# A graph-attention kernel whose walk over destination rows takes edge tiles column by column, one transfer for each step

## The reference

```
h_proj = einsum('nd,rde->rne', h, relation_weight)
t_r, h_r = h_proj[etype, src], h_proj[etype, dst]
att = sum(t_r * tanh(h_r + efeat), axis=-1)
a = segment_softmax(att, dst)
h_nb = segment_sum(h[src] * a[:, None], dst)
out = leaky_relu((h + h_nb) @ res_w1.T) + leaky_relu(h * h_nb @ res_w2.T)
x = layernorm(x + out)
```

## Time and profile before

| | |
|---|---|
| median of 3 runs | 8692.76 us (8691.06 to 8694.27) |
| the profiled execution's time | 8697.39 us |
| its span, first to last instruction | 8695.6 us |
| prologue, up to the first gather | 0 to 452 us |
| far chunks (gathers of sources and destinations) | 452 to 4009 us |
| near chunks (gathers of sources) | 4009 to 6211 us |
| node stages and second layer | 6211 to 8696 us |
| busy: PE, PEld, DVE, ACT, POOL | 59%, 54%, 73%, 38%, 59% |

### The profile page before, as it was taken

One profiled execution on the slowest core, in us unless ns is written; L12 is line 12 of the kernel. 1 busy time (PEld: TensorE's weight loads), 2 busy tenths in 40 slices (PEclk: granted clock), 3 DMA queues, 4 the chain that ended last, 5 costly groups with the idle time before them and its releaser, 6 DMA issues. The chain is left out here.

```text
span 8695.6 us, 134675 instructions
## 1 busy us (share of the span) xinstructions
PE 5099.5 (59%) x44411; PEld 4652.1 (54%) x44577; DVE 6318.7 (73%) x6282; ACT 3267.4 (38%) x4027; POOL 5097.0 (59%) x5165
## 2 busy tenths in 40 slices
PE   6657777777777777775000000000159999999995
PEld 2247676766766766774000000000158888888884
DVE  4546556556565565566777787777789999999997
ACT  3312122122122222222222222222257777777772
POOL 3777777777777777777777777777631121111114
PEclk8855555555555555555555555555559999999996
DMA  9978877878788777887444444444310000000001
GB/s 390 383 170 184 183 179 179 179 180 182 178 180 183 176 180 184 176 181 170 132 132 133 132 132 133 130 134 130 94 35 10 10 9 10 9 10 10 9 10 31
DMA packets 1216488, 1142.57 MB, mean 131 GB/s; under 512 B 993596, under 2 KB 1047422, under 8 KB 1203200
## 3 DMA queue, kind: packets, MB, share of 16 engines
q1 hardware_dynamic: 1036607, 754.44, 34.3%
q0 software_dynamic: 160592, 281.30, 14.7%
q10 hardware_dynamic: 19200, 105.87, 3.1%
HBM read 697.83 MB, written 444.96 MB: 131 GB/s over the span
## 5 line engine op out<-in xcount | busy, mean ns | idle before, releaser
L1543 POOL DMA_INDIRECT gs<-table,idx_s x3125 | 3011.1, 964 | 981.3 <-issue 964.5
L1851 PEld LDWEIGHTS banks<-win,pick 128*125 128x125 f32 x9900 | 2151.1, 332 | 341.5 <-issue 316.1
L1851 PE MATMUL banks<-win,pick 128*125 (+1 forms) x9900 | 2120.9, 413 | 190.9 <-DVE pick L1599 189.0
L765 ACT CAST columns<-ps_u 128x784 bf16<-128x784 f32 x1968 | 1577.8, 813 | 461.8 <-PE ps_u L795 416.1
L1547 POOL DMA_INDIRECT gd<-table,idx_d x1375 | 1363.0, 991 | 419.0 <-issue 419.0
L1835 PE MATMUL banks<-hi,lo 128*128 128x98 bf16 x3125 | 279.0, 283 | 2004.0 <-DVE hi L1586 2004.0
L1835 PEld LDWEIGHTS banks<-hi,lo 128*128 128x128 bf16 x3125 | 263.9, 146 | 2019.0 <-DVE hi L1586 2019.0
L647 POOL DMA_INDIRECT tile_row<-tile_rows,now x123 | 304.6, 2476 | 1749.7 <-PE ps_k L785 1690.6
L803 PE MATMUL ps_s<-parts,columns 128*128 128x192 bf16 x12054 | 1315.7, 248 | 0.4 <-ACT columns L765 0.4
L1620 DVE TENSOR_TENSOR gd<-gd,ef 128x1600 f32<-128x1600 f32 x55 | 100.4, 1826 | 1504.2 <-DMA gd<-table,idx_d 1504.2
L795 PE MATMUL ps_u<-hot_h,hot_l 125*128 125x98 bf16 x15744 | 1056.6, 210 | 193.0 <-DVE hot_h L711 184.4
(11 more groups left out here) (315 smaller groups left out, 5952.5 us busy)
## 6 DMA issues: line engine op xcount, KB each, us to landing
proj_d<-found SPq DMA_DIRECT2D x330, 512.0 KB
win<-table SPq DMA_DIRECT2D x660, 240.0 KB
table<-rows SPq DMA_DIRECT2D x98, 1536.0 KB, 9.7
sums<-rowbuf ACTq DMA_DIRECT2D x124, 825.0 KB
ef<-in_edge_attr_dram SPq DMA_DIRECT2D x125, 800.0 KB, 4.7
keyb<-step_keys SPq DMA_DIRECT2D x332, 234.4 KB, 5.4
gd<-proj_d SPq DMA_DIRECT2D x70, 800.0 KB, 6.1
gs<-table,idx_s POOLq DMA_INDIRECT x3125, 2.5
```

The lines of the kernel that those rows point to most:

```text
L765: nc.scalar.copy(columns[:, j % 2, i * UU:(i + 1) * UU, :].rearrange("p (b u) h -> p b (u h)", b=UB), ps_u[n % 2][:, :, 0:UU // UB * NB]). ...
L1543: pool.indirect_dma_start(out=gs[:, s, g, :], out_offset=None, in_=table_vec, in_offset=bass.IndirectOffsetOnAxis(ap=idx_s[:, s, g:g + 1], ...
L1851: nc.tensor.matmul(acc[k][0:MT, bass.ds(slots[t] * D, D)], pick[:, w, t * MT:(t + 1) * MT], win[:, w, bass.ds(at_w, 1), :].rearrange("p o ...
```

## The change

- FAR goes from 55 to 30. 25 chunks lose their destination gathers and become near chunks, of which there are now 95, and a partition has TPP = 19 tiles in the walk instead of 14.
- The walk goes over tiles column by column: first tile 0 of every partition, then tile 1 of every partition, and so on. Within a column the groups rise; from one column to the next they start again. So the windows of a block no longer are one stretch, and each of the 15 steps has its own window transfer of 128 partitions, with its own number from `group_list`. SyncE loads 16 numbers for each block (15 groups and the place of an output) from a small ring in SBUF that two transfers per chunk fill (`plan`).
- A near chunk needs only the columns up to its own, so the walk goes on beside the first 80 near chunks, two blocks in each. Far chunks take 7 and 8 blocks in turn. There are 385 blocks instead of 330.
- To make room, `keep` and `arg_ps` are smaller: the last of a chunk's 25 places is computed from SBUF, and the scan is in four pieces instead of two. One accumulator serves near blocks.
- Keys of later blocks are issued by ScalarE after its copy of `found`, no longer by SyncE. The picks of a far chunk stand mostly at its front.
- TensorE reads window t of a block at a fixed place.
- The prologue makes the longer lists; the group of each step comes from an extra column of `tile_keys`.

The core of the diff:

```diff
-FAR = 55
+FAR = 30
 K = 15
-PER = 6
-BLOCKS = PER * FAR
-UC = -(-(BLOCKS * K + 1) // P)
-KSLOTS, WSLOTS = 4, 3
+PER = (7, 8)
+WALKED = 80
+FAR_BLOCKS = FAR // 2 * sum(PER)
+BLOCKS = FAR_BLOCKS + 2 * WALKED
+UC = -(-((BLOCKS + 2) * K + 1) // P)
+WSLOTS = 3
...
-                    sp.dma_start(tile_keys.rearrange("(p k) e -> p (k e)", p=P), key_f[:, :]).then_inc(keys_out, 16)
+                    sp.dma_start(tile_keys.rearrange("(k p) e -> p k e", p=P), key_f).then_inc(keys_out, 16)
...
-            keep = banks[:, 2:4, :].rearrange("p b x -> p (b x)")[:, 0:WH * (1 + G)]
-            arg_ps = banks[:, 4:8, :].rearrange("p b x -> p (b x)")[:, 0:G * D].rearrange("p (g d) -> p g d", d=D)
-            acc = [banks[:, 4 + 2 * k:6 + 2 * k, :].rearrange("p b x -> p (b x)") for k in range(2)]
+            WT = (W + 3) // 4
+            keep, weight = banks[:, 2, 0:WT * (1 + G)], banks[:, 2, BANK - 32:BANK - 32 + G]
+            IN_PS = 3 * BANK // D
+            arg_ps = banks[:, 3:6, :].rearrange("p b (g d) -> p (b g) d", d=D)
+            acc = [v.rearrange("p b x -> p (b x)") for v in (banks[:, 6:8, :], banks[:, 3:5, :])]
...
-            windows = table.rearrange("(w a) c -> a w c", a=4 * PAIR_ROWS)
+            windows = table.rearrange("(w a) (v d) -> w v a d", a=4 * PAIR_ROWS, v=VECS)
-            proj_v = proj_d[:, 0:TILES, :].rearrange("e (p k) d -> p k e d", k=TPP)
+            proj_v = proj_d[:, 0:TILES, :].rearrange("e (k p) d -> p k e d", p=P)
...
+                    def plan(b, n, s):
+                        sp.dma_start(ring[0:1, s, 0:n, 0:K],
+                                     group_list[bass.ds(b * K + 1, n * K)].rearrange("(o b j) -> o b j", o=1, j=K)).then_inc(ring_in[s], 16)
+                        with nc.allow_non_contiguous_dma(reason="one number of each block"):
+                            sp.dma_start(ring[0:1, s, 0:n, K:K + 1],
+                                         cum_list[bass.ds(b * K + LEAD - 2 * K, n * K)].rearrange("(o b j) -> o b j", o=1, j=K)[:, :, 0:1]).then_inc(ring_in[s], 16)
...
-                    def inputs(b, k):
-                        g0 = nc.values_load(sp_tab[0:1, bass.ds(2 * b, 1)], engines=[mybir.EngineType.SP],
-                                            min_val=0, max_val=N // 4 - 1, skip_runtime_bounds_check_because=MADE)
-                        if not isinstance(b, int) or b >= WSLOTS:
-                            sp.wait_ge(found_mm, b - WSLOTS + 1)
-                            sp.sem_inc(sp_past, 1)
-                        for h in range(2):
-                            sp.dma_start(win[64 * h:64 * h + 64, k, :, :],
-                                         windows[:, bass.ds(g0, K), 2 * h * D:(2 * h + 1) * D]).then_inc(win_in[k], 16)
+                    def inputs(b, x, s, slot, free, landed, k):
+                        _, numbers = nc.values_load_multi_w_load_instructions(
+                            ring[0:1, s, x, :], engines=[mybir.EngineType.SP], min_val=0, max_val=N // 4 - 1,
+                            skip_runtime_bounds_check_because=MADE)
+                        if not isinstance(b, int) or b >= WSLOTS:
+                            sp.wait_ge(found_mm, free)
+                            sp.sem_inc(sp_past, 1)
+                        for t in range(K):
+                            sp.dma_start(win[:, slot, t, :],
+                                         windows[bass.ds(numbers[t], 1), 0:VECS:2, :, :].rearrange("o v a d -> (o v) a d")).then_inc(landed, 16)
+                        if not isinstance(b, int) or b >= 2:
+                            outputs(b - 2, k, numbers[K])
...
                     def projected(c, s, k, c5):
                         sp.wait_ge(slot_ready, c + 1)
                         sp.sem_inc(sp_past, 1)
+                        sp.wait_ge(found_out, 16 * (FIRST_COLUMN + MORE_COLUMN * k))
+                        sp.sem_inc(sp_past, 1)
                         sp.dma_start(gd[:, s, :, :], proj_v[:, bass.ds(k, 1), G * c5:G * c5 + G, :].rearrange("p o e d -> p (o e) d")).then_inc(pd_in[s], 16)
...
+                        if walked:
+                            plan(near_block(c + 1, 0), 2, 1 - s)
+                            sp.wait_ge(ring_in[s], 32 * (FAR // 2 + 5 * n + m // 2 + 1))
+                            sp.sem_inc(sp_past, 1)
+                            for j in range(2):
+                                b = near_block(c, j)
+                                inputs(b, j, s, j, b - 1, win_near[j], (FAR_BLOCKS + j) % 2)
...
-                        nc.scalar.copy(found[:, k, :], acc[k]).then_inc(found_ready, 1)
+                        nc.scalar.copy(found[:, k, :], acc[a]).then_inc(found_ready, 1)
+                        if next_b is not None:
+                            act.dma_start(keyb[:, slot, :],
+                                          step_list[bass.ds((next_b * K + 1) * MT, K * MT)].unsqueeze(0).to_broadcast([P, K * MT])).then_inc(key_in[slot], 16)
...
-                        for w0, w1 in ((0, WH), (WH, W)):
+                        for w0, w1 in ((0, WT), (WT, 2 * WT), (2 * WT, 3 * WT), (3 * WT, W)):
...
-                            at_w = nc.s_assert_within(slots[0] - slots[t] + t, 0, K - 1, skip_runtime_bounds_check_because=MADE) if t else 0
-                            nc.tensor.matmul(acc[k][0:MT, bass.ds(slots[t] * D, D)], pick[:, w, t * MT:(t + 1) * MT],
-                                             win[:, w, bass.ds(at_w, 1), :].rearrange("p o d -> p (o d)"), start=False, stop=False)
+                            nc.tensor.matmul(acc[a][0:MT, bass.ds(slots[t] * D, D)], pick[:, w, t * MT:(t + 1) * MT],
+                                             win[:, w, t, :], start=False, stop=False)
```

More of the change, by code:

```diff
@@ new lines, in far @@
+                    def far(c, s, i, q, at, n):
+                        b = block_no(q, at)
+                        if isinstance(c, int) and c == 0:
+                            plan(0, n, 0)
+                        plan(b + n, PER[1] if n == PER[0] else PER[0], 1 - s)
+                        sp.wait_ge(ring_in[s], 32 * (i + 1))
+                        sp.sem_inc(sp_past, 1)
+                        for x in range(n):
+                            inputs(b + x, x, s, (at + x) % WSLOTS, b + x - WSLOTS + 1, win_in[(at + x) % WSLOTS], (at + x) % 2)
+                        sp.wait_ge(tanh_arg, c + 1)
+                        sp.sem_inc(sp_past, 1)
+                        load(c + 2, s)
@@ L1779, in chunk @@
                         act.wait_ge(tanh_arg, k + 1)
-                        nc.scalar.activation(arg_t, arg_t, ACT.Tanh).then_inc(tanh_done, 1)
+                        for _, _, arg_t in args:
+                            last = nc.scalar.activation(arg_t, arg_t, ACT.Tanh)
+                        last.then_inc(tanh_done, 1)
                         if far:
-                            take_found(PER * c + 1, 1)
+                            far_found(q, at + blocks - 5)
+                        if walked and not first:
+                            near_found(c - 1, 1)
                         act.wait_ge(exp_arg, k + 1)
@@ L1855, in walk, with far @@
                             pe.wait_ge(found_ready, b)
-                        nc.tensor.matmul(acc[k][:, 0:D], ident[:, :], found[:, 1 - k, bass.ds(slots[K] * D, D)],
+                        nc.tensor.matmul(acc[a][:, 0:D], ident[:, :], found[:, 1 - k, bass.ds(slots[K] * D, D)],
                                          start=False, stop=True).then_inc(found_mm, 1)
-                    histogram(0)
-                    for j in range(PER):
-                        walk(0, j)
-                    with pe.Fori(1, FAR) as c:
+                    def far(c, s, i, q, at, n):
@@ L1863, in _, with near @@
                         histogram(c)
-                        for j in range(PER):
-                            walk(c, j)
-                    with pe.Fori(FAR, CHUNKS) as c:
+                        for x in range(n):
+                            b, slot = block_no(q, at + x), (at + x) % WSLOTS
+                            walk(b, (at + x) % 2, (at + x) % 2, slot, win_in[slot], 16 * K * slot_turn(q, at + x), b - 1)
+                    def near(c):
+                        histogram(c)
+                        for j in range(2):
+                            b = near_block(c, j)
+                            walk(b, (FAR_BLOCKS + j) % 2, 0, j, win_near[j], 16 * K * (c - FAR + 1), b)
@@ L1867, in _ @@
+                    far_chunks(pe, far)
+                    with pe.Fori(FAR, FAR + WALKED) as c:
+                        near(c)
+                    with pe.Fori(FAR + WALKED, CHUNKS) as c:
                         histogram(c)
```

383 lines of the change are left out of this document (217 added, 166 removed).

## The result

The changed kernel takes 11,294.5 us, the median of 4 runs (11,289.2 to 11,298.3), against 8,693.5 us for the kernel before (8,691.1 to 8,694.9): a ratio of 1.2992, 95% interval 1.2969 to 1.3014. It is 2,601 us slower. The forecast was slower, 13,500 us, with 8,450 to 17,100 as its range; the forecast's own range began at 10,100. The profiled execution took 11,295.2 us over a span of 11,293.4.

What follows compares the result with a forecast made beforehand. GpSimd's gathers bound the kernel before; after the change, two DMA engines: 3411 us fixed + 5490 (30 far chunks at 183) + 4560 (80 walked near at 57) = 13,460, say 13,500; range 8,450 to 17,100, own range 10,100 to 17,100.

Steps and rivals of the forecast that it cites:

- two DMA engines carrying every window: Window transfers of the walk: outermost dimension two puts every step on the same two of 16 engines; 13,500 us, chance 0.62.
- Packet time: Window transfers: a full DMA engine passes one 256-byte packet each 22 ns (18 to 30), 21.1 us a block.
- Other traffic on the two engines: Gathers, row stores, keys and outputs on the windows' engines: 25 us added a far chunk, 15 a walked near chunk.
- The pause between blocks: Sync queue between one block's window issues and the next: no term in the two-engine sum, the engines taken as never idle.
- DMA share: Sign for the forecast: share low, about 0.2 to 0.3, in both edge stages, with TensorE waiting for window transfers.
- A landing far over 2.5 us: Sign for the forecast: a step's window transfer would take far more than 2.5 us to land.
- Rival 1: Sync queue sets the far pace with all 16 engines: block 12.25 us, far chunk 93.5, total 8712 to 10,080; chance 0.19.
- the load: Sync queue, each block: loading 16 numbers takes 3.9 us, a figure from TensorE's queue; low end 0.3.
- the step: Sync queue, each of 15 window issues a block: 0.51 us from start to start, bounds 0.45 to 0.81.
- Rival 2: All 16 engines and a cheap sync queue, step under 0.506 us: faster, 8510 down to 7850 us; chance 0.16.
- only just fits: TensorE in a far chunk: 7.5 blocks, 62 us plus 2.2 for the histogram, in 64.7; no cost if windows come in time.
- Prologue and end: Before the first gather and after the last: 5 us added to the prologue, giving 457; end unchanged at 2486.

Runs made afterwards that it cites:

- e1: Changed kernel with the window source's dimensions swapped so 64 table rows are outermost, pick lanes renumbered to match: 9,528.6 us, ratio to before 1.0960.
- e8: e5's two queues with the source order of the changed kernel, outermost dimension two again: 11,610.5 us, one run.
- e3: Changed kernel with half of each vector's rows moved, 480 packets instead of 960 on each of two engines, windows zeroed once: 9,782.9 us, one run.
- e4: Changed kernel with only the first of 15 window transfers a block issued, windows zeroed once: 8,005.2 us, one run.
- e5: e1 with ScalarE's queue loading the numbers and issuing the window transfers of steps 8 to 14: 8,115.1 us, ratio to before 0.9331.
- e2: Changed kernel with each step's window cut into two transfers of 64 partitions, 64 rows outermost, thirty a block: 12,942.0 us, one run.

## Why the prediction was right, and where its sizes were off

**The mechanism was right.** The forecast's case, two DMA engines carrying every window, is what the runs show: one change of the order in which the same rows are named takes 1,766 us off (e1), relieving the queue takes nothing off (e8), and halving the packets takes 1,512 us off (e3). The Trainium skill (DMA: Bandwidth & Descriptors, "Why a DMA increments its semaphore by 16 and not by 1") gives the rule that the prediction weighed, the largest count up to 16 that divides the slowest dimensions of both sides; the runs agree with it in every case tried (2 against 64 outermost rows: 11,294.5 against 9,528.6 us). No view here lists the 16 engines one by one. But never more than 4 packets are in flight where the rule says 2 engines, and up to 29 where it says 16 (the kernel before), about two an engine in both; and where windows move alone the share is 0.16, or 2.6 engines by a measure that overlaps and reads 1.37 at its peak, which makes about two.

**Packet time.** 22 ns from the earlier trace rows, bounds 18 and 30. The ceiling of 36 GB/s is 141 packets a microsecond, so on two engines one each 14.2 ns. All three figures were too high. The weak step is 30/1.37: the 30 ns were read in a load in which other transfers took part, where a packet lasts longer (27 ns on average for those of 256 bytes in the far stretch before, 18 in the changed kernel).

**Other traffic on the two engines.** 25 us a far chunk and 15 near were added. Over the far blocks (all but the first and last five, from the start of a block's first window issue to the end of its last) the 15 issues last 14.8 us on average, against 13.7 for the windows alone at the ceiling. The difference, some 1.1 us a block or 8 a far chunk, is as much as other traffic stretches them.

**The pause between blocks** stood at nothing. The forecast let the two engines run without a break. But from the last window issue of a block to the first of the next the sync queue has the output to issue and 16 numbers to load, and at times the edge load and the plan: 3.7 us on average in far blocks, and for part of it the two engines run dry (the gap around 2224 us above). A far block starts every 18.5 us: 13.7 for the windows, 1.1 of stretch, 3.7 of pause.

So the total of 13,500 is a packet time and a traffic term that are too large and a pause that is missing. Far came out at 183 us a chunk instead of 139.2 (30 x 44 = 1,314 us too much) and near at 57 instead of 46.4, the mean from the end of far, 480.2 + 30 x 139.2 = 4656, to the last window issue at 8369.8 over 80 chunks (80 x 10.6 = 848 us too much). 13,460 - 1,314 - 848 = 11,298 against 11,295 in the profiled execution. The low end of the forecast's own range, 18 ns and the rest hidden, was 130 us a far chunk and 34.6 near. That far comes within 7% of 139.2 is partly luck: its 4 ns too much a packet stand in for the pause. Near it is a quarter under.

**DMA share.** 0.2 to 0.3 was expected, 0.35 and 0.52 measured: the sign of it, low shares in both stages with TensorE waiting for windows, was right, and so was the sign of stretched issues. A landing far over 2.5 us did not show: TensorE starts on a block at 2223.41, 3.0 us after the end of its last window issue at 2220.38. The issues are held back instead.

**The sync queue (Rival 1)** was real and stood right behind. Its terms, against e1: the load 1.7 to 1.9 us (I took 3.9, "the load's 3.9 is from another engine" was the objection that held), the step 0.73 (taken 0.51, bounds 0.45 to 0.81), so a block without waits 13.8 instead of 12.25, a far chunk 110.2 instead of 93.5, and near 35.2 ((6605.9 - 3786.7) / 80) instead of 31.2, since two blocks, 27.6 us, and what the queue waits for no longer fit under it. Rival 1's range of 8,712 to 10,080 holds e1's 9,529. How the two limits combine can be read from the far blocks. In e1 a block is 11.0 us of issues and 3.5 of pause, in the changed kernel 14.8 and 3.7. During the issues the longer one hides the other, 13.7 us of windows over 11.0 of queue. The pause comes on top in both. That is why mending the layout alone takes only the 3.9 us a block off, and mending the queue alone nothing.

**Rival 2** needed a step under 0.506 us; the step is 0.73 with nothing in its way. Its floor of 7,850 was not reached even with one window transfer a block: e4 stands at 8,005.

**TensorE** "only just fits" was wrong by about 4 us a far chunk (68.5 against 64.7, e4), 115 us in all, unseen in the result because windows were later still.

**Prologue and end.** The first gather starts at 478.9 instead of 452.0, 27 us later where 5 were taken; I have no run that tells why. What follows the start of the last gather is 11,295.2 - 8,809.0 = 2,486 us, as predicted.

Where the 2,601 us come from, then, by the sum: fewer gathers would have given 847 back (8,697 to 7,850). Blocks that come at the windows' pace, pause included, cost 30 x (139.2 - 64.7) = 2,235 far and 80 x (46.4 - 31.2) = 1,216 near, and 2,235 + 1,216 - 847 = 2,604.

The idea of the change is sound once both are mended: e5 keeps its walk, its 30 far chunks and its 128-partition steps and beats the kernel before by 6.7%. Of e5's distance to e4, 110 us, most is far: 72.0 against 68.5 us a chunk. The wait of found behind ScalarE's own queue (72.6 us in 500, e5) points at the seven issues; no run tells it apart from the rest.

## What to carry to other kernels

When transfers are merged, write down the outermost dimension of the longer side of the new one: a merge that halves the issues but turns 64 outermost rows into two can cost far more than it saves. The cure here was another order of dimensions, with the consumer's indices renumbered. The sign in a profile is a DMA share that falls while an engine waits for DMA, and issues whose time spreads above their usual value. Behind such a limit look for the next one before mending it: count the queue's instructions at their start-to-start time, 0.73 us here for a transfer with a computed address, and count apart what the queue does between two groups of transfers, since engines that are fed only during the issues stand idle in between. Deal issues over both queues only when they run unhindered: in e8 the ones that were held back also stopped ScalarE's work behind them.

## What the runs showed of the hardware

- A window issue with a computed address of 128 partitions takes 0.538 us on the sync queue, 0.73 from start to start (e1); of 64 partitions 0.468 and 0.66 (e2). Half of the partitions are hardly cheaper. A lone issue of the changed kernel's layout took 0.608 (e4, median). In the kernel before an issue of 64 partitions took 0.63 with the DMA share at 0.8.
- In the far stretch, where they moved alone, transfers with an outermost dimension of two stood at 36 GB/s in 256-byte packets, with at most 4 of them in flight; the same bytes with 64 rows outermost came in bursts of up to 184 GB/s, with up to 23 in flight (e1).
- ScalarE's queue issues the same transfer in 0.552 us, 0.73 from start to start (e5).
- The load of 16 numbers into registers took 1.9 us on the sync queue and 3.9 on TensorE's; here the element types differ too, and no run separates the two.
- Issues are held back when the engines that serve them are full: the same instruction went from 0.538 us with almost no spread to a median of 0.704 on the sync queue, and seven steps from 5.1 to 13.9 us on ScalarE's.
